# One reordering of the opening of an eight-core attention and ternary feed-forward kernel: weight loads, ternary passes, first masks and a layer norm

## The reference, cut to what matters

```python
xn  = layernorm(x)                       # x: 2 x 16384 x 1024, float32
q, k, v = xn @ w_q + b_q, xn @ w_k + b_k, xn @ w_v + b_v   # 16 heads of 64
# each token attends to 7 neighbours (3 each side), softmax over the valid ones
att = softmax(q . k_window / 8) . v_window
a   = att @ w_o + b_o
scale = max(mean(|weight|), 1e-5)        # feed-forward weight, 1024 x 1024
w_t = clip(round(weight / scale), -1, 1) # ternary
f   = xn @ (w_t * scale).T
out = x + a + f
```

## Time and profile before

| what | value |
|---|---|
| time before, three runs | 678.42 us median (677.29 to 795.39) |
| profiled execution, its own time | 678.97 us |
| span of its slowest core (core 2) | 677.1 us |
| PE busy | 629.9 us, 93% of the span |
| DVE busy | 434.5 us, 64% |
| ACT busy | 374.4 us, 55% |
| POOL busy | 88.1 us, 13% |
| mean granted TensorE clock of core 2 | 0.985 |
| chain that ended last | PE 85%, DMA 5%, issue 3%, DVE 3%, ACT 3% |

### The profile page before, as it was taken

The page is one execution under the profiler, slowest core; times in us unless marked ns, Lnnn a source line. Parts: engine busy times, 40 slices in busy tenths (PEclk is TensorE's granted clock), DMA queues, the critical chain, the costliest instruction groups (busy, mean ns, idle before and its releaser), DMA issues.

```text
span 677.1 us, 11621 instructions; the slowest of 8 cores (671.6 to 677.1 us)
## 1 busy us (share of the span) xinstructions
PE 629.9 (93%) x3827; PEld 296.8 (44%) x3890; DVE 434.5 (64%) x534; ACT 374.4 (55%) x1418; POOL 88.1 (13%) x52
## 2 busy tenths in 40 slices
PE   1889986999999999999999999999899999999997
PEld 1344433444444444444444444444344444455543
DVE  6335888777666666666756676666666755566663
ACT  3453665555565545556555655555556555566573
POOL 1203000421111110111111111001011111111110
PEclk9989987999999999999999999999799999999999
DMA  8999997686554655556542665564453433334523
GB/s 192 206 207 283 154 154 164 161 204 140 126 139 127 156 141 139 124 114 131 134 103 84 146 136 141 140 154 112 89 114 86 100 82 94 92 97 106 146 78 93
DMA packets 129946, 91.17 MB, mean 135 GB/s; under 512 B 107872, under 2 KB 116192, under 8 KB 129888
## 3 DMA queue, kind: packets, MB, share of 16 engines
q1 hardware_dynamic: 121440, 82.05, 48.4%
q0 software_dynamic: 8448, 8.39, 8.9%
HBM read 55.82 MB, written 16.78 MB: 107 GB/s over the span
## 4 chain that ended last, share of the span: by engine, by line
PE 85%; DMA 5%; issue 3%; DVE 3%; ACT 3%; POOL 0%; DVEq 0%; ACTq 0%; SPq 0%; POOLq 0%
PE p_p L310 17%; PE p_p L335 16%; PE p_p L292 15%; PE p_f L460 15%; PE p_f L476 14%; PE p_s L363 3%; PE p_a L423 3%; DMA wq_b<-wq 3%; ACT sm L393 2%; DMA et<-en 1%; DVE sm L378 1%; DMA x<-x 1%; DVE en L406 1%; PE p_s L460 1%; PE p_p L553 1%
## 5 line engine op out<-in xcount | busy, mean ns | idle before, releaser
L393 ACT ACTIVATE sm<-sm,nmx 122x128 f32<-122x128 f32 x544 | 210.6, 392 | 15.7 <-DVE nmx L385 15.7
L489 POOL TENSOR_TENSOR xr<-xr,brow 128x1024 f32<-128x1024 f32 x32 | 75.4, 2360 | 507.7 <-DMA xr<-x 452.5
L292 PE MATMUL p_p<-xnt,wq_b 128*128 128x488 bf16 (+1 forms) x576 | 126.2, 367 | 4.0 <-ACT xnt L270 3.7
L310 PE MATMUL p_p<-xnt,wk_b 128*128 128x494 bf16 (+1 forms) x576 | 123.1, 360 | 0.0
L335 PE MATMUL p_p<-wv_b,xnt 128*128 128x512 bf16 x513 | 117.4, 381 | 4.9 <-issue 4.8
L300 ACT ACTIVATE qt<-p_p,bq 128x488 bf16<-128x488 f32 (+1 forms) x72 | 46.1, 640 | 135.6 <-PE p_p L292 135.5
L460 PE MATMUL p_f<-wft_b,xnt 128*128 128x512 bf16 x494 | 114.1, 385 | 0.5 <-DVE xr L494 0.4
L476 PE MATMUL p_f<-wo_b,att 128*128 128x512 bf16 x468 | 107.0, 379 | 5.5 <-issue 4.3
L378 DVE TENSOR_TENSOR sm<-p_s,mk_sb 122x1024 f32<-122x1024 f32 x68 | 82.9, 1219 | 34.1 <-PE p_s L363 34.1
L393 ACT ACTIVATION_READ_ACCUMULATOR sm<-sm,nmx 122x1 f32 x544 | 104.4, 192 | 0.0
L348 ACT CAST v<-p_p 128x512 bf16<-128x512 f32 x68 | 39.0, 576 | 103.1 <-PE p_p L335 103.1
(11 more groups left out here) (62 smaller groups left out, 277.4 us busy)
## 6 DMA issues: line engine op xcount, KB each, us to landing
xr<-x SPq DMA_DIRECT2D x32, 512.0 KB, 5.5
x<-x SPq DMA_DIRECT2D x31, 512.0 KB, 5.5
out<-xr SPq DMA_DIRECT2D x31, 512.0 KB, 3.4
wq_b<-wq POOLq DMA_DIRECT2D x4, 512.0 KB, 13.9
wk_b<-wk POOLq DMA_DIRECT2D x4, 512.0 KB, 15.5
xr<-wft SPq DMA_DIRECT2D x4, 512.0 KB, 11.4
wv_b<-wv POOLq DMA_DIRECT2D x4, 512.0 KB, 15.9
wo_b<-wo POOLq DMA_DIRECT2D x4, 512.0 KB, 25.7
```

The costliest lines, as they stand in the source:

```text
L292: q.do("tensor", lambda e, k=k: e.matmul(bank[:, 0:m], w_b["wq"][:, k * H + 128 * c:k * H + 128 * c + 128], rows_of(b, k, BQ * b + 3, m), ...
L310: q.do("tensor", lambda e, k=k: e.matmul(bank[:, 0:m], w_b["wk"][:, k * H + 128 * c:k * H + 128 * c + 128], rows_of(b, k, BQ * b, m), star ...
L393: q.do("scalar", lambda e, h=h: e.activation(sm[hf][0:TQ, KW * h:KW * h + KW], sm[hf][0:TQ, KW * h:KW * h + KW], AF.Exp, bias=nmx[hf][0:TQ ...
L489: q.do("gpsimd", lambda e: e.tensor_tensor(xr[t % NR][:, :], xr[t % NR][:, :], brow[:, :], ALU.add), ("xrb", t))
```

## The change

On POOL's list the second half of `wk` (two loads) moves behind a wait, which is now for feed-forward piece 4 in place of piece 5; `wv` and `wo` follow directly. The sum of `wf_scale` becomes `wf_sum`, ahead of the first keys; the rest of `wf_scale` moves from behind three keys of block 1 to directly behind `k_job(0, 3)`. The first scores and mask come one key job of block 1 later, and so do the second ones. One ternary pass pair comes ahead of the first mask; the second goes behind it. `weights(0, 0)` moves ahead of the second mask. The exponentials of half 1 are spread over three key jobs. Ternary pieces 6 and 7 in the order of processing are split: one between the masks of step 0, one after `weights(1, 0)`. The layer norm of step 0 (`normalise(8)`, the DMA transposes of tiles 7 and 8, the load of x tile 11) and `stats(9)`, `rstd(9)` move from step 0 into step 1, behind the mask of `scores(2, 0)`.

```diff
-        def wf_scale():
+        def wf_sum():
             q.need("vector", *[("wabs", k) for k in range(8)])
             q.do("vector", lambda e: e.tensor_reduce(
                 wab[:, 8:9], wab[:, 0:8], AX.X, ALU.add), "wsum")
+
+        def wf_scale():
             q.need("tensor", "wsum", t_last[7])
@@ -590,11 +592,11 @@
         weight_load("wk", 0)
-        weight_load("wk", 1)
         q.need("sync", ("w", "wk", 0, 0))
         for k in range(8):
             wf_load(k)
-        q.need("gpsimd", ("wf", 5))
+        q.need("gpsimd", ("wf", 4))
+        weight_load("wk", 1)
         weight_load("wv", 0)
@@ -618,12 +620,9 @@
         for k in range(8):
             wf_abs(k, "vector")
+        wf_sum()
         for c in range(4):
             k_job(0, c, "scalar")
-        scores(0, 0)
-        mask_max(0, 0)
-        for c in range(3):
-            k_job(1, c, "scalar")
         wf_scale()
@@ -631,21 +630,26 @@
-        some_terns(0, 2)
+        some_terns(0, 1)
+        k_job(1, 0, "scalar")
+        scores(0, 0)
+        mask_max(0, 0)
+        some_terns(1, 2)
         stats(8)
         some_terns(2, 4)
-        k_job(1, 3, "scalar")
+        k_job(1, 1, "scalar")
         for c in range(4, 8):
             exps(0, 0, range(2 * c - 8, 2 * c - 6))
             k_job(0, c, "scalar")
         rstd(8)
+        weights(0, 0)
+        k_job(1, 2, "scalar")
         scores(0, 1)
         mask_max(0, 1)
-        weights(0, 0)
         some_terns(4, 6)
-        for c in range(4, 6):
+        for c in range(3, 6):
             k_job(1, c, "scalar")
-            exps(0, 1, range(4 * c - 16, 4 * c - 12))
+            exps(0, 1, ((0, 1), (2, 3, 4), (5, 6, 7))[c - 3])
@@ -694,6 +698,12 @@
                 scores(n, 0)
                 mask_max(n, 0)
+                if s == 0:
+                    some_terns(6, 7)
+                if s == 1:
+                    layer_norm_step(0)
+                    stats(stats_of_step(1))
+                    rstd(stats_of_step(1))
                 v_job(n, 0)
@@ -706,13 +716,13 @@
-                if not qk:
+                if not qk and s >= 1:
                     layer_norm_step(s)
...
-            if after is not None:
+            if after is not None and s >= 1:
                 stats(after)
@@ -721,19 +731,19 @@
                 weights(n, 0)
+            if s == 0:
+                some_terns(7, 8)
             if n < NW:
                 e_transpose(n, 0)
             if t is not None:
                 f_proj(t)
-            if s == 0:
-                some_terns(6, 8)
...
-            if after is not None:
+            if after is not None and s >= 1:
                 rstd(after)
```

## The result

| | before | changed |
|---|---|---|
| median of 6 runs each | 678.04 us | 680.54 us |
| ratio of the runs, 95% interval | 1 | 1.0034 [1.0022, 1.0047] |
| profiled execution, its own time | 678.97 us | 681.05 us |
| span of its slowest core | 677.1 us | 679.5 us (core 5) |
| span of its fastest core | 671.6 us | 671.5 us |

The time lies inside the range of 672.8 to 681.0, but the sign was wrong. One execution of before took 795.39 us and stands outside the comparison.

A forecast was written before the change was run, and what follows sets the result against it. PE is full from 170 us, so only when it becomes full counts. Of 5.2 us gained at scores (2,1), tile 7's wait left 1.9: 678.97 - 1.9 = 677.1, and 0.55 lower for the median, 676.5; range 672.8 to 681.0.

The forecast's parts named there:

- The moved layer norm: Step 1 on DVE: `normalise(9)` waits 6 us for tile 7's transpose, to 113.1; bias row at 119.6, against 118.96.
- Scores one key job later: First two scores on PE: both waits of 0.92 us go, 1.8 us off PE; cost on ACT 0, at worst 1 us.
- Scale and thresholds: Scale's tiny matmul on PE at 61.8: sums done at 57, cost 0; 1.3 us if loads were not faster.
- The weight wk, second half: Before `k_job(0, 4)`: landed at 65.3, needed at 65.6; cost taken 0, bounds 0 and 4.9 us.
- rival three: At `k_job(0, 4)`, second half of `wk` late: worst 3.0 us slower, 681.4; middle about 679; chance 0.20.
- One us for each us: At `k_job(0, 4)`: each us that piece 4 lands later than 51.3 costs one us.
- First transposed weights: SP's first transpose: issued at 76.6 in place of 83.11, takes 10.5 us, lands at 87.1, ahead of its user at 90.6.
- rival two: First transpose held by `wo`, landing at 93.6 as before; scores (2,1) at 104.5, time 679.5; chance 0.15.
- landed before 90: Sign that the forecast is right: the first transpose issued near 77 and landed before 90.
- Rival one: Tile 7's transpose lands before 108 or its wait is hidden; the 5.2 us at 106.56 stay: 673.2; chance 0.18.
- Clock: At `f_proj(0)`: the clock it may get back (5.77 to 3.63) is hidden in PE's wait; nothing added.

The follow-up runs named there:

- e6: Changed kernel with the layer norm of step 0 back in step 0 and three key jobs of block 1, not one, ahead of `k_job(0, 4)`: 674.21 us, 0.9900 of before.
- e11: Changed kernel with three key jobs of block 1 ahead of `k_job(0, 4)` in place of one, layer norm left in step 1: 679.02 us, 0.9998 of before.
- e2: Changed kernel with the layer norm of step 0, `stats(9)` and `rstd(9)` back in step 0: 678.48 us, 0.9965 of before.
- e5: Changed kernel with the second half of `wk` issued early and the layer norm of step 0 back in step 0: 678.89 us, 0.9963 of before.
- e1: Changed kernel with the second half of `wk` issued directly behind the first half, ahead of the feed-forward pieces: 683.06 us, 1.0025 of before.
- e4: Changed kernel with the second half of `wk` issued early and the transpose of tile 7 issued in step 0: 680.85 us, 0.9998 of before.
- e10: e6 with `wo` issued on POOL only when the transposes of window 0 have landed: 683.23 us, 1.0059 of before.
- e3: Changed kernel with only the DMA transpose of tile 7 issued in step 0 again: 680.72 us, 0.9992 of before.
- e12: e6 with the second half of `wk` waiting for feed-forward piece 2 in place of piece 4: 674.56 us, 0.9901 of before.

## Why the prediction was wrong, point by point

The time was to fall by 1.9 us and rose by 2.5, so 4.4 us are to be explained. Covering the wait for `wk` gives back 0.36%, 2.4 us. The moved layer norm cost 4.1 to 4.7 us where I had 3.3, which is another 0.8 to 1.4 us. The rest, 0.6 to 1.2 us, is within the uncertainty of the ratios. Nor do the two parts simply add: with both undone (e6) the time falls by 1.34% against the changed kernel, where singly it falls by 0.36% (e11) and 0.69% (e2).

- **Scores one key job later.** Right: no idle time before 62.94 and 76.65. The opening's new order as a whole gains 0.37% (e5); no run separates this part from the other reorderings.
- **Scale and thresholds.** Right in the changed kernel: sums done at 57.9 (forecast 57), no wait at 61.04.
- **The weight wk, second half: this step failed.** "Cost taken: 0; bounds 0 and 4.9 us." It came to 3.12 us on the slowest core. POOL's issue came at 52.1, not 51, and the second load took 15.2 us in place of 13.5: it landed at 68.1, 2.8 us behind the 65.3 of the forecast. The key jobs had begun 0.6 us earlier than in the earlier trace rows, and the slack was 0.3 us: 2.8 + 0.6 - 0.3 = 3.1. So the term had 0.3 us of slack against a spread of 3.2 us between cores, and I took its middle for all eight. The slowest core is by choice one where it was short. With 3.1 added to the forecast the later times fit: scores (2,1) 101.3 + 3.1 against 103.95, `normalise(9)` 113.1 + 3.1 against 116.28, `f_proj(1)` 123.4 + 3.1 against 126.84. Some luck is in this: tile 7's transpose was issued 2.0 us later than forecast and took 1.1 us longer (9.9 in place of 8.8), which happens to make 3.1. Where the wait was absent (core 1) `f_proj(1)` came within 0.8 us of the forecast. It was rival three (chance 0.20). Its middle was 0.5 us slower than before and its worst 3.0; the measured 2.5 is nearer the worst, as the wait came with the undersized layer norm. "One us for each us" was too little as well: behind such a wait the clock took up to 2.9 us more.
- **What that wait proves, and what not.** Covering it with key jobs gives back 0.36% (e11 against the changed kernel), the whole of the loss against before, but not the 0.28% that the forecast had as a gain. Loading `wk` early doesn't (e1, e4, e5): the wait moves to the scale. So I read the late `wk` as the symptom of an order in which `k_job(0, 4)` comes too early. e11 also puts exponentials and the second scores behind more key jobs; no run has the cover without that.
- **First transposed weights.** It was issued at 76.63 as forecast, and took 14.6 us, not 10.5. It landed at 91.2, before `wo` ended at 96.7: it wasn't held until `wo` ended, so rival two fell. The Trainium skill, "DMA: Bandwidth & Descriptors" (section on queues, rings and completion order), describes DMA engines that take turns between queues; the 91.2 against 96.7 agrees with that. But sharing is dear (e10: 4.5 and 3.3 us alone). My sign "landed before 90" failed by that. The second transpose landed at 97.1, 0.4 us behind the last `wo` load, and by that one alone the two readings can't be told apart. It cost PE 3.64 us, which I hadn't listed; it lay beside DVE's chain.
- **The moved layer norm.** The wait for tile 7 was forecast at 6 us and measured at 6.12. I let it take back 3.3 of 5.2 us gained. The runs put the move at 0.60% to 0.69%, 4.1 to 4.7 us: with it undone the changed order is faster than before. Mechanism right, size too small. Only 0.42% goes with the transpose (e3). The other 0.27% goes with the rest of the move, which I had counted as if it were free once DVE had stood waiting. One thing that I had called no loss is visible: `rstd(9)` and two V evictions stood before `att_evict(1,0)` on ACT, which came at 109.35, and PE waited 1.93 us for it.
- **Rival one** (all of 5.2 us kept if tile 7 doesn't wait) fell with the changed kernel's own trace: tile 7 landed at 116.2, not before 108. Its price is not refuted by the 0.9992 of e3, where the wait for `wk` was still there. Core 4 of that run, which waited only 0.4 us for it, had an opening of 86.6 us, 4.7 below the mean of before, in a set of runs in which before took 2.8 us more.
- **Clock.** On core 5 `f_proj(0)` took 3.63 us in place of 5.77, but the slower clock had only moved: the V job at 97.81 took 5.29 us at a granted clock of 0.68, and the bias matmuls at 110.51 took 5.31, where 16 such matmuls take 3.63 at the full clock. So that core got nothing back from the clock in the opening, and core 7 lost 2.9 us more by it.

Open: why the cores differ in when their second half of `wk` lands, while the openings before were within 1.8 us of each other. Cores 4, 5 and 7 lost and 1 and 3 gained in one profiled execution; other cores did in e2. No run varied what the cores share. Open as well is why three cores kept the full clock after a wait of 3.1 to 3.2 us for `wk` and others didn't.

## What to carry to other kernels

A term with slack of a few tenths of a microsecond on a DMA isn't zero when the slowest of eight cores counts: price it at the latest core, and add what the clock loses behind the wait. When a load is late, ask which work with its operands already there can go ahead of it, before asking to load it sooner; here the earlier load only made another one late. And follow a moved step through every list it passes: the transpose of tile 7 was a small DMA, but behind three loads it held DVE 6 us.

## What the runs showed of the hardware

- A DMA transpose of one window's half took 3.3 to 4.5 us without, and 11.1 to 14.6 us with, POOL's converting weight loads in flight.
- POOL's loads landed about 3.2 to 4 us apart once the queue was full (`wv` between 68.1 and 80.9, `wo` between 80.9 and 96.7, on core 5). In the changed kernel nothing was in flight on POOL's queue from 42.0, where the first half of `wk` had landed, to 52.1, where piece 4 let the next load go. The last load landed 3.7 us later than before, though the sum of bytes was the same: about a third of the queue's idle time wasn't made up.
- After PE had stood idle for 3.0 to 5.8 us, nine of twelve cores (the changed kernel, e2, e3) ran the next five key jobs in 9.85 to 11.42 us in place of 8.49. Over the 11.41 us of core 7 the granted clock was 0.74, with 0.50 from 68 to 72. Where key jobs filled the wait (e6, e11, e12) no core did.
